# A product's operands: S sums moved from VectorE to GpSimd, and the set-up's order changed

## The reference

```python
def cond(x, language, W, Wr, A, B):          # x: 32 x 64 x 1024, so 2048 tokens of 1024
    base = einsum('btd,od->bto', x, W)
    logits = einsum('btd,ed->bte', x, Wr) + 5.0 * one_hot(language, 8)
    topw, topi = top_k(logits, 2)
    gates = sum(one_hot(topi, 8) * softmax(topw)[..., None], axis=-2)
    h = einsum('btd,erd->bter', x, A)        # 8 experts, rank 16
    return base + 2.0 * einsum('bter,bte,eor->bto', h, gates, B)

def ffn(x, W, b, A, Bm, Wr):                 # 4 experts, rank 8
    base = einsum('bsi,oi->bso', x, W) + b
    gates = softmax(einsum('bsi,ei->bse', x, Wr))
    lora = einsum('bser,eor->bseo', einsum('bsi,eri->bser', x, A), Bm)
    return base + einsum('bse,bseo->bso', 2.0 * gates, lora)

out = x + ffn(cond(x, ...), ...)
```

## Time and profile before

| | us |
|---|---|
| median of 3 runs (334.72 to 334.98) | 334.88 |
| the profiled execution | 334.72 |
| its span in the profile | 332.5 |
| TensorE busy | 326.1 |
| VectorE busy | 213.5 |
| ScalarE busy | 119.4 |
| GpSimd busy | 6.2 |

### The profile page before, as it was taken

One profiled execution on the slowest core, in us unless ns is written; L12 is line 12 of the kernel. 1 busy time (PEld: TensorE's weight loads), 2 busy tenths in 40 slices (PEclk: granted clock), 3 DMA queues, 4 the chain that ended last, 5 costly groups with the idle time before them and its releaser, 6 DMA issues.

```text
span 332.5 us, 5493 instructions
## 1 busy us (share of the span) xinstructions
PE 326.1 (98%) x2059; PEld 321.7 (97%) x2059; DVE 213.5 (64%) x470; ACT 119.4 (36%) x238; POOL 6.2 (2%) x14
## 2 busy tenths in 40 slices
PE   7999999998999999999999999999999999999996
PEld 7999999998999999999999999999999999999995
DVE  2989999779899879156446725634763572565421
ACT  4972836475148325032212412411341250322111
POOL 1000005000000000000000000000000000000000
PEclk9999999999999999999999999999999999999999
DMA  7994000033000004301500500240070033003003
GB/s 251 417 408 134 2 2 0 11 117 128 0 2 0 2 1 127 125 0 46 206 0 0 220 33 0 71 181 0 0 252 0 0 122 131 0 1 126 1 0 126
DMA packets 8188, 26.96 MB, mean 81 GB/s; under 512 B 1038, under 2 KB 2062, under 8 KB 8176
## 3 DMA queue, kind: packets, MB, share of 16 engines
q1 hardware_dynamic: 8032, 26.80, 22.0%
q10 hardware_dynamic: 144, 0.01, 0.0%
HBM read 18.42 MB, written 8.39 MB: 81 GB/s over the span
## 4 chain that ended last, share of the span: by engine, by line
PE 92%; DMA 3%; DVE 2%; ACT 1%; issue 0%; SPq 0%; DVEq 0%; ACTq 0%
PE sums L1032 91%; DMA in<-part 2%; DMA stage<-tokens 1%; DVE st_low L670 1%; PE sums L1221 1%; PE sums L1246 1%; DVE rows L673 0%; DVE a_low L670 0%; DVE b_low L670 0%; ACT st_high L468 0%; ACT a_high L468 0%; DVE c_plain L740 0%; DVE rows L765 0%; DVE rows L1018 0%; ACT b_high L468 0%
## 5 line engine op out<-in xcount | busy, mean ns | idle before, releaser
L1032 PE MATMUL sums<-b_high,a_high 128*128 128x256 f32 (+1 forms) x224 | 45.8, 288 | 1.4 <-DVE c_plain L740 1.3
L1032 PE MATMUL sums<-ct_low,st_high 128*128 128x428 f32 x128 | 45.6, 357 | 0.0
L1032 PE MATMUL sums<-ct_high,st_high 128*128 128x428 f32 x128 | 45.6, 356 | 0.0
L1032 PE MATMUL sums<-ct_high,st_low 128*128 128x428 f32 x128 | 45.6, 356 | 0.0
L1032 PE MATMUL sums<-b_high,a_low 128*128 128x256 f32 (+1 forms) x224 | 45.5, 286 | 0.0
L1032 PE MATMUL sums<-b_low,a_high 128*128 128x256 f32 (+1 forms) x224 | 45.4, 286 | 0.0
L1032 PEld LDWEIGHTS sums<-b_high,a_high 128*128 128x128 f32 x224 | 35.0, 190 | 2.0 <-issue 1.4
L1032 PEld LDWEIGHTS sums<-b_high,a_low 128*128 128x128 f32 x224 | 34.9, 190 | 0.0
L1032 PEld LDWEIGHTS sums<-b_low,a_high 128*128 128x128 f32 x224 | 34.9, 190 | 0.0
L1032 PE MATMUL sums<-t_high,s_high 128*128 128x384 f32 x96 | 32.4, 338 | 0.0
L1032 PE MATMUL sums<-t_high,s_low 128*128 128x384 f32 x96 | 32.4, 337 | 0.0
(11 more groups left out here) (130 smaller groups left out, 670.5 us busy)
## 6 DMA issues: line engine op xcount, KB each, us to landing
stage<-tokens SPq DMA_DIRECT2D x16, 512.0 KB, 3.5
out<-rows SPq DMA_DIRECT2D x14, 512.0 KB, 3.7
in<-part SPq DMA_DIRECT2D x7, 585.0 KB, 8.3
in<-part SPq DMA_DIRECT2D x4, 777.0 KB, 15.2
in<-part SPq DMA_DIRECT2D x4, 265.0 KB, 18.0
out<-rows SPq DMA_DIRECT2D x4, 192.0 KB, 2.1
c_plain<-gate_proj SPq DMA_DIRECT2D x1, 544.0 KB, 17.5
c_plain<-mix_rows SPq DMA_DIRECT2D x1, 392.0 KB
```

What stands on the lines that cost most here:

```text
L1032: return nc.tensor.matmul(out_, lhs, rhs, start=start, stop=stop, skip_group_check=True)
```

## The change

`add_s` moves from VectorE's queue to GpSimd's. There it stands behind the three identity sums: `add_s(0)` first, then a loop over the other pairs. In this loop it waits for the splits of the pair before's sums (`s_split`), since they are read from the same buffer, and for `v_ready` of the pair before. Both waits for the token tiles stay.

In the set-up, `round_tail(C11)` and `split_tail(C11)` move from before P6's first step to behind step 22 (ScalarE) and behind `add_out(P6)` (VectorE). On VectorE `split_step(26)` moves ahead of `add_out(P7)`, `split_t(T1)` ahead of `split_tail(C22)`, and `make_t` for T3 behind T2 and the split of B22. On ScalarE `round_tail(C22)` moves behind `round_t(T1)`.

```diff
--- before.py
+++ after.py
@@ -460,6 +460,35 @@
                 nc.gpsimd.tensor_tensor(c_plain[:, C22, dt, a:a + P], c_plain[:, C22, dt, a:a + P], ident[:, :],
                                         ALU.add).then_inc(c22_ident, 1)
 
+            def minus(dst, a, b):
+                return nc.gpsimd.tensor_tensor(dst, a, b, ALU.subtract)
+
+            def add_s(j, first=False):
+
+                def block_of(odd, h):
+                    return stage[:, odd, h * HALF * P:(h + 1) * HALF * P]
+
+                def s_of(n):
+                    return (s_first if first else s_plain)[:, n, :, :].rearrange("p k c -> p (k c)")
+
+                if not first:
+
+                    pool.wait_ge(s_split, 4 * j)
+                    pool.wait_ge(v_ready, j)
+                pool.wait_ge(x_here[0], 16 * j + 16)
+                pool.wait_ge(x_here[1], 16 * j + 16)
+
+                nc.gpsimd.tensor_tensor(s_of(S1), block_of(1, 0), block_of(1, 1), ALU.add).then_inc(s1_made, 1)
+                pool.wait_ge(s1_made, j + 1)
+                minus(s_of(S2), s_of(S1), block_of(0, 0)).then_inc(s_made, 2)
+                minus(s_of(S3), block_of(0, 0), block_of(1, 0)).then_inc(s_made, 1)
+                pool.wait_ge(s_made, 4 * j + 2)
+                minus(s_of(S4), block_of(0, 1), s_of(S2)).then_inc(s_made, 1)
+
+            add_s(0, first=True)
+            with pool.Fori(1, PAIRS) as j:
+                add_s(j)
+
         @block.scalar
         def _(act):
             act.dma_start(lang_i[:, :], language).then_inc(lang_here, 16)
@@ -554,8 +583,6 @@
 
             act.wait_ge(c0_split, 1)
             copy_out(Q_P5, C22)
-            act.wait_ge(c11_made, 1)
-            round_tail(C11)
             for n in range(16, 20):
                 round_step(n)
 
@@ -573,6 +600,8 @@
             round_step(21)
             round_x(0, 1)
             round_step(22)
+            act.wait_ge(c11_made, 1)
+            round_tail(C11)
             round_step(23)
             round_block(B11, C11)
             round_step(24)
@@ -581,12 +610,12 @@
             round_tail(C12)
             round_step(26)
             round_step(27)
-            act.wait_ge(added_out, 8)
-            round_tail(C22)
 
             act.wait_ge(op_split, STEPS_F)
             act.wait_ge(t1_made, 1)
             round_t(T1, C11)
+            act.wait_ge(added_out, 8)
+            round_tail(C22)
             round_block(B22, C22)
             act.wait_ge(t2_made, 1)
             round_t(T2, C11)
@@ -750,24 +779,6 @@
                 low_part(s_low[:, n, :, :], plain[:, n, :, :], s_high[:, n, :, :]).then_inc(s_split, 1)
 
             TAIL_ORDER = (C11, C12, C22, C21)
-
-            def add_s(j, plain):
-
-                def block_of(odd, h):
-                    return stage[:, odd, h * HALF * P:(h + 1) * HALF * P]
-
-                def s_of(n):
-                    return plain[:, n, :, :].rearrange("p k c -> p (k c)")
-
-                dve.wait_ge(x_here[0], 16 * j + 16)
-                dve.wait_ge(x_here[1], 16 * j + 16)
-
-                nc.vector.tensor_tensor(s_of(S1), block_of(1, 0), block_of(1, 1), ALU.add).then_inc(s1_made, 1)
-                dve.wait_ge(s1_made, j + 1)
-                minus(s_of(S2), s_of(S1), block_of(0, 0)).then_inc(s_made, 2)
-                minus(s_of(S3), block_of(0, 0), block_of(1, 0)).then_inc(s_made, 1)
-                dve.wait_ge(s_made, 4 * j + 2)
-                minus(s_of(S4), block_of(0, 1), s_of(S2)).then_inc(s_made, 1)
 
             def split_tail(c):
                 dve.wait_ge(ct_rounded, TAIL_ORDER.index(c) + 1)
@@ -848,7 +859,6 @@
                 .then_inc(vec, 1)
             VEC_START = 3
 
-            split_tail(C11)
             split_step(16)
             for k in range(HALF):
                 make_t4(k)
@@ -866,11 +876,11 @@
             split_step(21)
             split_x(0, 1)
             split_step(22)
-            add_s(0, s_first)
 
             dve.wait_ge(copied_out, 4 * (Q_P3 + 1))
             add_out(Q_P6, C12, 0, C12)
             add_out(Q_P6, C12, 1, C12)
+            split_tail(C11)
             split_step(23)
             split_block(B11, C11)
 
@@ -879,21 +889,21 @@
             split_step(24)
             split_step(25)
             split_tail(C12)
+            split_step(26)
 
             dve.wait_ge(c22_ident, 3)
             add_out(Q_P7, C22, 0, C22)
             add_out(Q_P7, C22, 1, C22)
-            split_step(26)
             split_step(27)
 
+            split_t(T1, C11)
             split_tail(C22)
 
             dve.wait_ge(added_out, 8)
-            make_t(C12, C22, C12, t3_made)
-            split_t(T1, C11)
-
             make_t(C11, C22, C11, t2_made)
             split_block(B22, C22)
+
+            make_t(C12, C22, C12, t3_made)
 
             add_out(Q_P4, C21, 0, C21)
             add_out(Q_P4, C21, 1, C21)
@@ -1004,7 +1014,6 @@
                 nc.vector.tensor_tensor(rows[:, 1, WIDE:2 * WIDE], bank(BANK_C), rows[:, 1, WIDE:2 * WIDE], ALU.add)\
                     .then_inc(r22_read, 1)
                 if not last:
-                    add_s(j + 1, s_plain)
                     split_x(j + 1, 1)
 
                 dve.wait_ge(r22_read, j + 1)
```

## The result

The changed kernel takes 339.96 us (median of 4 runs, 339.46 to 342.86), the kernel before 334.93 (334.72 to 337.09). The ratio is 1.0118, with a 95% interval of 1.0075 to 1.0162: slower by about 4 us by the ratio and by 5.0 by the medians, where 334.0 was forecast. Some executions of every kernel, the one before included, take some 2.4 us more outside the span (334.96 for a span of 332.9, 341.54 for one of 337.0), and an execution more than 1.5% above the fastest of its kernel, as the 342.86 here, doesn't enter a ratio.

A forecast was written before the change was run, and what follows sets the result against it. TensorE was taken as the bound, its only wait behind the start-up 1.49 us before P7. B21 left 1.29, less 0.43 collision, so 0.86; the loop added 0: 334.88 - 0.86 = 334.0 us, range 333.4 (333.6 less 0.2) to 335.0.

The forecast's parts named there:

- The stall and its worth: TensorE's wait before P7's first matmul, until add_out(P6) empties the bank, with its restart: 1.49 us, all to go.
- So a dense chain on VectorE starves GpSimd: Rule read from the first identity sum near 51, 4.03 us long: back-to-back VectorE operations with two SBUF inputs keep GpSimd out.
- So S1 waits until then: Pair 0's first GpSimd sum waits until VectorE's split chain from 69.99 ends at 74.80, and ends at 75.96.
- 0.43 us of collision behind P7: Third sum, S3, runs until 78.60 and delays VectorE's operation after P6's add_outs, due at 78.17, by 0.43 us.
- GpSimd wins against VectorE once more inside the gapless work: Slower rival: from 78 to 116 one more sum holds VectorE, costing 1.24; shift -0.38, time 335.3 us; chance 0.10.
- An add_out beside GpSimd: Assumed that GpSimd can work beside an add_out, which has one input in PSUM and one in SBUF.
- One sum: Duration of one 128x512 sum on GpSimd: taken as 1.24 us, between bounds of 1.10 and 1.67.
- Part 2: VectorE's new set-up order: worked out up to B21's split, leaving a shift of 1.29 less the collision, 0.86 us.
- the shift: How much earlier everything behind the product on B21 comes: 1.29 us without a collision, 0.86 with 0.43 of it.
- the arrival at `add_out(P7)`: VectorE reaches it in the set-up at 87.74 plus the collision; without a collision, next to no stall at P4.
- the bound at B21: Ends last: B21's split ends at 116.40 plus the collision; TensorE can use it about 0.10 later, wants it at 116.30.
- Part 3: add_s in the loop on GpSimd: sums are on time for ScalarE, so the loop changes by 0.

The follow-up runs named there:

- b22_late_too: Kernel before, add_s(0) on VectorE behind split_step(27), B21's split swapped with T3's, split_step(26) ahead of add_out(P7), B22's split behind first pair's v_ready: ratio 0.9971.
- sums_as_memset: Changed kernel with pair 0's four GpSimd sums replaced by constants written by memset: ratio 0.9980 to the kernel before.
- sums_after_p7: Changed kernel with one more wait: pair 0's sums on GpSimd begin only when add_out(P7) is done; ratio 1.0100 to the kernel before.
- part2_alone: Kernel before with only the set-up's new order, add_s staying on VectorE, for pair 0 behind split_step(22): ratio 1.0035.
- loop_alone: Kernel before with the sums of the other seven pairs on GpSimd, add_s(0) on VectorE and the old set-up order: ratio 0.9994.

## Why the prediction was wrong

**The stall and its worth: right.** 1.49 us were said to hang on P7's wait. b22_late_too removes it and gains 1.49; in sums_as_memset the first tail product comes 36.45 after the marker, before 37.85.

**The step that failed: "So a dense chain on VectorE starves GpSimd", and with it "So S1 waits until then".** From one sum near 51 the prediction made a rule for the chain from 70.24. There GpSimd got in after each of VectorE's operations: S1 ran at 71.47, not at 74.80, and all four sums stood on the way to P7 instead of beside TensorE's pace. The term was 0.43 us of collision behind P7 and measured 4.4 us before it, 1.06 to 1.10 for each sum. It is more than the 2.6 us that `add_s(0)` had cost on VectorE itself. The page of the Trainium skill ("SBUF — State Buffer", "Who interferes with whom") that was quoted speaks of a lock for one instruction, not of one held over a chain; the turns at 70 agree with it, with each side waiting out one operation of the other. The prediction let one row decide how the lock passes on. T3's 2.57 us, in which it does not pass, and the two splits that S1 waits out in sums_after_p7 are not told by that page.

**The rival with the right sign had the right price and the wrong place.** "GpSimd wins against VectorE once more inside the gapless work" priced an extra sum at 1.24, but looked for it from 78 to 116 and gave it 0.10. That all four could win from 70 on was not among the cases, so the range ended at 335.0.

**The fall of the clock was missing.** No term stood for it: 1.50 us in the profiled execution, half of what was lost between the two points. The kernel before had a wait of 1.26 with the clock at 1.00 throughout, and the prediction never asked what a longer one would do.

**An add_out beside GpSimd: right.** The operation at 155.68, with one PSUM operand, isn't slowed. That was assumed without a row. An `add_out` itself does not fall beside a sum in these traces.

**One sum: right.** 1.29 alone for 1.24.

**Part 2: right.** In sums_as_memset, where nothing collides, the shift is 1.26 for 1.29, and the arrival at `add_out(P7)`, VectorE's idle time for T1 (1.56 for "some 1.6") and the bound at B21 are as worked out. The 0.37 us lost behind VectorE's last operation there had no term in the prediction. part2_alone shows that the same order costs 0.42 where VectorE is not relieved.

**Part 3: right.** loop_alone: 227.36 against 227.37.

## What to carry to other kernels

Work that leaves VectorE for GpSimd has not left VectorE where both read two operands from SBUF: here each 128x512 sum on the way to P7 still held VectorE for 1.06 to 1.10 us, where VectorE would have needed 0.61 for it. Move such work only to where VectorE idles, reads PSUM, or has slack, or move it to a later place in VectorE's own queue and take out of the way there what is needed last. And when a wait of TensorE may grow, price what the clock does behind it, not the wait alone.

## What the runs showed of the hardware that was not expected

- GpSimd and VectorE take turns, operation by operation, in all sums at 70, in the loop and in T4, but not in T3 (sums of 2.58 and 3.90 us where one takes 0.42 alone, beside unchanged VectorE operations), nor at 90 in sums_after_p7 (2.30, behind two splits). This is left open.
- Memsets of 128x512 on GpSimd don't disturb VectorE's splits at all: 0.68 and 0.70 beside four of them.
- TensorE's clock stayed at 2.4 GHz behind waits of 0.96, 1.26 and 1.93 us before P7, and went to 1.2 GHz for some 3.4 us behind waits of 2.26 (at the tails), 2.78 and 3.03. That is one profiled execution of each; of the other executions of those last three kernels some have a mean clock of 0.998 or more.
- A span ends 3.18 to 3.27 us behind VectorE's last operation in thirteen traces, and 3.59 to 3.93 in the five in which GpSimd writes pair 0's sums. This is left open too.
